# A gated attention and FFN block on one core: the last tile's second half of gate and up in other PSUM banks, and its quantised hidden rows turned by TensorE in quarters

## The reference

```python
x = x + tanh(g_xattn[0]) * cross_attention(layernorm(x), ctx, Wq, Wk, Wv, Wo, bo)   # 8 heads of 64
x = x + tanh(g_ffn[0])   * ffn(layernorm(x), w_gate, w_up, w_down)

def bitlinear(x, w):     # act_quant: rows to 127 levels by the row's largest magnitude
    return act_quant(x) @ weight_quant(w).T          # weight_quant: -1, 0, 1 times the mean magnitude
def ffn(x, w_gate, w_up, w_down):
    g = bitlinear(x, w_gate); u = bitlinear(x, w_up) # 512 -> 2048
    h = square(relu(g)) * u
    return bitlinear(h, w_down)                      # 2048 -> 512
```

## Time and profile before

| | |
|---|---|
| median of 3 runs | 1275.16 us (1270.67, 1275.16, 1582.71) |
| profiled execution, its own time | 1274.61 us |
| its span | 1272.8 us, mean granted TensorE clock 0.983 |
| busy | PE 1211.8 us (95%), DVE 1047.2 (82%), ACT 692.0 (54%), POOL 310.4 (24%) |
| DMA | 124.55 MB, mean 98 GB/s |

### The profile page before, as it was taken

One profiled execution on the slowest core, in us unless ns is written; L12 is line 12 of the kernel. 1 busy time (PEld: TensorE's weight loads), 2 busy tenths in 40 slices (PEclk: granted clock), 3 DMA queues, 4 the chain that ended last, 5 costly groups with the idle time before them and its releaser, 6 DMA issues.

```text
span 1272.8 us, 18729 instructions
## 1 busy us (share of the span) xinstructions
PE 1211.8 (95%) x6040; PEld 783.4 (62%) x6136; DVE 1047.2 (82%) x2142; ACT 692.0 (54%) x803; POOL 310.4 (24%) x299
## 2 busy tenths in 40 slices
PE   7765999999999999999999999999999999999995
PEld 5544666666666666666666666666666666666652
DVE  4967888888888888888888888888888888888873
ACT  3853455554566555554565545564575545555453
POOL 1024122222243222222243122212243222221210
PEclk9897999999999999999999999999999999999997
DMA  9740433323332344323332244322333233322322
GB/s 392 267 156 21 130 91 88 73 76 82 91 87 66 75 117 141 79 70 81 91 87 70 77 121 134 87 66 74 91 87 76 73 83 91 87 70 78 75 59 58
DMA packets 205186, 124.55 MB, mean 98 GB/s; under 512 B 173930, under 2 KB 173930, under 8 KB 202593
## 3 DMA queue, kind: packets, MB, share of 16 engines
q1 hardware_dynamic: 204573, 120.00, 34.6%
q10 hardware_dynamic: 580, 4.20, 1.1%
HBM read 57.86 MB, written 24.35 MB: 65 GB/s over the span
## 4 chain that ended last, share of the span: by engine, by line
PE 81%; DVE 5%; POOL 3%; issue 2%; ACT 2%; DMA 0%; DVEq 0%; POOLq 0%; ACTq 0%; SPq 0%
PE gu_ps L1036 32%; PE o_ps L1021 16%; PE y_ps L1049 15%; PE s_ps L56 15%; PE s_ps L1009 3%; POOL v_sb L853 1%; DVE half_max L1120 1%; POOL probs L863 1%; DVE staged L1115 1%; ACT staged L945 0%; ACT x_marked L958 0%; DVE stats L1145 0%; DVE x L1143 0%; DVE x_max L1155 0%; DVE probs L1095 0%
## 5 line engine op out<-in xcount | busy, mean ns | idle before, releaser
L1036 PE MATMUL gu_ps<-w_gate,xq_t 128*128 128x512 bf16 x990 | 238.2, 383 | 7.4 <-DVE staged L1115 4.9
L1049 PE MATMUL y_ps<-w_down,hq_t 128*128 128x512 bf16 x1023 | 233.1, 381 | 5.6 <-DMA hq_t<-staged 5.4
L1036 PE MATMUL gu_ps<-w_up,xq_t 128*128 128x512 bf16 x963 | 235.0, 380 | 3.2
L1021 PE MATMUL o_ps<-v_sb,pt_high 128*128 128x512 f32 (+1 forms) x640 | 213.9, 415 | 1.7 <-DVE pt_low L1105 1.7
L1115 DVE TENSOR_TENSOR staged<-staged,gu_ps 128x1024 f32<-128x1024 f32 x128 | 155.5, 1215 | 62.9 <-ACT staged L928 57.9
L858 POOL TENSOR_TENSOR rstd<-var_eps,neg_half 128x1 f32<-128x1 f32 x128 | 100.2, 783 | 399.6 <-DVE var_eps L1082 280.0
L958 ACT ACTIVATE x_marked<-centred,x_scale 128x512 f32<-128x512 f32 x64 | 46.2, 722 | 261.6 <-DVE x_scale L1162 261.6
L56 PE MATMUL s_ps<-a_sb,xf_high 128*128 128x308 f32 x1024 | 187.1, 305 | 0.0
L1049 PEld LDWEIGHTS y_ps<-w_down,hq_t 128*128 128x128 bf16 x1024 | 100.6, 98 | 127.9 <-issue 8.3
L1036 PEld LDWEIGHTS gu_ps<-w_up,xq_t 128*128 128x128 bf16 x1024 | 100.6, 98 | 122.3 <-issue 2.7
L56 PEld LDWEIGHTS s_ps<-a_sb,xf_high 128*128 128x128 f32 x1024 | 159.7, 188 | 5.8 <-issue 0.5
(11 more groups left out here) (106 smaller groups left out, 1431.3 us busy)
## 6 DMA issues: line engine op xcount, KB each, us to landing
xf_sb<-in_x_feat SPq DMA_DIRECT2D x64, 256.0 KB, 2.7
x_sb<-in_x_tok SPq DMA_DIRECT2D x64, 256.0 KB, 2.8
y<-staged SPq DMA_DIRECT2D x64, 256.0 KB, 2.0
staged<-in_wg_t SPq DMA_DIRECT2D x4, 1024.0 KB, 15.5
staged_up<-in_wu_t SPq DMA_DIRECT2D x4, 1024.0 KB, 23.4
staged<-in_wd_t ACTq DMA_DIRECT2D x4, 1024.0 KB, 6.8
a_scr<-a_out SPq DMA_DIRECT2D x12, 308.0 KB, 4.4
a_raw<-a_scr SPq DMA_DIRECT2D x3, 1232.0 KB, 5.7
```

Of the source, the lines that this page charges most:

```text
L1021: last = nc.tensor.matmul(o_ps[:, :], pt[0:rows, P * c:P * (c + 1)], v_sb[0:rows, v, c, :], start=(c == 0 and pt is pt_high and v == 0), s ...
L1036: last = nc.tensor.matmul(gu_ps[:, m, q, :], xq_t[:, s.par(0), c, :], w[:, c, cols], start=(c == 0), stop=(c == DC - 1))
L1049: last = nc.tensor.matmul(y_ps[:, :], hq_t[:, c, :], w_down[:, c, :], start=(c == 0), stop=(c == FC - 1))
```

## The change

In step 63 half 1 of gate goes to `s_ps` and half 1 of up to the two gate banks of `gu_ps`. The wait for DVE's multiply of half 0 is dropped; gate waits for the last reader of `s_ps` (`pt_low_done`) and up for ACT's relu of half 0 (`relu_done[0]`). ACT's relu and DVE's multiply of half 1 read from the new places.

In step 64 the hidden rows of tile 63 take another way. The constant is now `MARKED`, ROUND plus 16384, so that the low 16 bits of the float32 result hold the integer plus 16384. DVE computes three quarters of 512 columns, ACT the fourth (`mark_last`). PE transposes each quarter straight from those low halves, read as bfloat16 with a stride of two, in four 128 by 128 transposes (`turn_last`) into a bank of its own (`o_ps`, the two of `s_ps`, one of `gu_ps`). ACT takes quarters 0 and 1 and DVE quarters 2 and 3 out of PSUM as 16-bit integers, less 16384, into `hq_t` (`take_last`). PE then runs the 16 down matmuls, waiting for each quarter (`down_last`). The two DMA transposes, the two ACT and one DVE operations that took ROUND off, and the two ACT operations of 1024 columns are gone for this tile. A second identity matrix, in bfloat16, is made by POOL at the start (one more memset and one more select), 256 bytes per partition of SBUF, allocated ahead of nearly all other tiles.

```diff
+        kept.ident_b = sb("ident_b", [P, P], BF16)
...
+        last_gate_ps, last_up_ps = pt_ps, gate_ps
+        last_turned_ps = [bank[:, 0:256].bitcast(BF16) for bank in (o_ps, s_ps[:, 0, :], s_ps[:, 1, :], gu_ps[:, 1, 0, :])]
+        h_bits = h_marked[:, :].bitcast(BF16).rearrange("p (n two) -> p n two", two=2)
...
 SP
-                    if s.has(-1):
+                    if s.has(-1) and not s.opens(TILES):
                         turn_hidden(s, -1, 0)
                         turn_hidden(s, -1, 1)
...
 ACT
+                    at_end = s.opens(TILES - 1) and n == 1
+                    if at_end:
+                        act.wait_ge(square_done[0], TILES)
+                    nc.scalar.activation(relu, last_gate_ps if at_end else gate_ps, ACT.Relu).then_inc(relu_done[n], 1)
...
+                def mark_last():
+                    act.wait_ge(h_scale_done, TILES)
+                    nc.scalar.activation(h_marked[:, 1536:FFN], hidden[:, 1536:FFN], ACT.Copy, bias=MARKED,
+                                         scale=h_scale[:, 0:1]).then_inc(last_marked[3], 1)
+                def take_last(q):
+                    act.wait_ge(last_turned[q], 1)
+                    act.wait_ge(down_done, TILES - 1)
+                    nc.scalar.activation(hq_t[:, 4 * q:4 * (q + 1), :], last_turned_ps[q].bitcast(I16).rearrange("p (c n) -> p c n", c=4),
+                                         ACT.Copy, bias=-LOW_MARK).then_inc(last_ready[q], 1)
...
 PE
-                    wait(pe, hidden_done[1 - n], s.count(n))
+                    at_end = s.opens(TILES - 1) and n == 1
+                    if not at_end:
+                        wait(pe, hidden_done[1 - n], s.count(n))
...
+                        target = gu_ps[:, m, :, :]
+                        if at_end:
+                            pe.wait_ge((pt_low_done, relu_done[0])[m], TILES)
+                            target = (s_ps[:, :, :], gu_ps[:, 0, :, :])[m]
...
+                def turn_last(q):
+                    pe.wait_ge(last_marked[q], 1)
+                    for c in range(4):
+                        at = 512 * q + P * c
+                        last = nc.tensor.transpose(last_turned_ps[q][:, P * c:P * (c + 1)], h_bits[:, at:at + P, 0], ident_b[:, :])
+                    last.then_inc(last_turned[q], 1)
+                def down_last():
+                    pe.wait_ge(y_done, TILES - 1)
+                    for q in range(4):
+                        pe.wait_ge(last_ready[q], 1)
+                        for c in range(4 * q, 4 * (q + 1)):
+                            last = nc.tensor.matmul(y_ps[:, :], hq_t[:, c, :], w_down[:, c, :], start=(c == 0), stop=(c == FC - 1))
                     last.then_inc(down_done, 1)
...
 DVE
                     if s.has(1):
                         probs_low(s, 1)
+                    if s.opens(TILES):
+                        for q in range(3):
+                            mark_last(q)
                     if s.has(-2):
                         finish(s, -2)
+                    if s.opens(TILES):
+                        for q in range(2, 4):
+                            take_last(q)
```

More of the change, by code:

```diff
@@ L11 @@
 BF16 = mybir.dt.bfloat16
+I16 = mybir.dt.int16
 P = 128
@@ L45 @@
 ROUND = float(3 << 22)
+LOW_MARK = 16384.0
+MARKED = ROUND + LOW_MARK
 CENTRED_MIN = EPS * EPS**0.5
@@ L253, in _ @@
                 nc.gpsimd.memset(ident_f[:, :], 0.0).then_inc(ident_zeroed, 1)
-                pool.wait_ge(ident_zeroed, 1)
-                nc.gpsimd.affine_select(out=ident_f[:, :], in_=ident_f[:, :], compare_op=ALU.not_equal, fill=1.0, base=0,
-                                        pattern=[[-1, P]], channel_multiplier=1).then_inc(ident_ready, 1)
+                nc.gpsimd.memset(ident_b[:, :], 0.0).then_inc(ident_zeroed, 1)
+                pool.wait_ge(ident_zeroed, 2)
+                for ident in (ident_f, ident_b):
+                    nc.gpsimd.affine_select(out=ident[:, :], in_=ident[:, :], compare_op=ALU.not_equal, fill=1.0, base=0,
+                                            pattern=[[-1, P]], channel_multiplier=1).then_inc(ident_ready, 1)
                 for n in range(2):
@@ L551, in run_tiles @@
 def run_tiles(nc, x_tok, x_feat, out, a_scr, v_scr, kept):
-    ident_f, neg_half = kept.ident_f, kept.neg_half
+    ident_f, ident_b, neg_half = kept.ident_f, kept.ident_b, kept.neg_half
     w_gate, w_up, w_down, staged = kept.w_gate, kept.w_up, kept.w_down, kept.staged
@@ L660, in run_tiles @@
         down_done, y_done = sem("down_done"), sem("y_done")
+        last_marked = [sem(f"last_marked{q}") for q in range(4)]
+        last_turned = [sem(f"last_turned{q}") for q in range(4)]
+        last_ready = [sem(f"last_ready{q}") for q in range(4)]
         ones_placed = sem("ones_placed")
@@ L921, in relu_half @@
                         wait(act, weight_done, 1)
-                    nc.scalar.activation(relu, gate_ps, ACT.Relu).then_inc(relu_done[n], 1)
+                    at_end = s.opens(TILES - 1) and n == 1
+                    if at_end:
+                        act.wait_ge(square_done[0], TILES)
+                    nc.scalar.activation(relu, last_gate_ps if at_end else gate_ps, ACT.Relu).then_inc(relu_done[n], 1)
                 def square_half(s, n):
@@ L963, in step @@
                         probs_high(s, 1)
-                    if s.has(-1):
+                    if s.opens(TILES):
+                        mark_last()
+                        take_last(0)
+                        take_last(1)
+                    elif s.has(-1):
                         mark_hidden(s, -1)
@@ L1035, in gate_up @@
                             for c in range(DC):
-                                last = nc.tensor.matmul(gu_ps[:, m, q, :], xq_t[:, s.par(0), c, :], w[:, c, cols],
+                                last = nc.tensor.matmul(target[:, q, :], xq_t[:, s.par(0), c, :], w[:, c, cols],
                                                         start=(c == 0), stop=(c == DC - 1))
@@ L1051, in down @@
                     last.then_inc(down_done, 1)
+                def turn_last(q):
[10 more added lines that the diff above has]
+                            last = nc.tensor.matmul(y_ps[:, :], hq_t[:, c, :], w_down[:, c, :], start=(c == 0), stop=(c == FC - 1))
+                    last.then_inc(down_done, 1)
                 def step(s):
@@ L1063, in step @@
                         gate_up(s, 1)
-                    if s.has(-1):
+                    if s.opens(TILES):
+                        for q in range(4):
+                            turn_last(q)
+                        down_last()
+                    elif s.has(-1):
                         down(s, -1)
@@ L1114, in hidden_half @@
                     wait(dve, h_marked_done[n], s.before(0))
-                    nc.vector.tensor_tensor(hidden[:, cols], relu_sq, up_ps, ALU.mult).then_inc(hidden_done[n], 1)
+                    at_end = s.opens(TILES - 1) and n == 1
+                    nc.vector.tensor_tensor(hidden[:, cols], relu_sq, last_up_ps if at_end else up_ps,
+                                            ALU.mult).then_inc(hidden_done[n], 1)
                 def top_half(s, n):
@@ L1178, in unmark_hidden, with mark_last, take_last @@
                     nc.vector.tensor_scalar(hq[:, 0:HALF], h_marked[:, 0:HALF], -ROUND, None, ALU.add).then_inc(hq_done[0], 1)
+                def mark_last(q):
+                    dve.wait_ge(h_scale_done, TILES)
+                    dve.wait_ge(hq_done[1], TILES - 1)
+                    cols = slice(512 * q, 512 * (q + 1))
+                    nc.vector.tensor_scalar(h_marked[:, cols], hidden[:, cols], h_scale[:, 0:1], MARKED,
+                                            ALU.mult, ALU.add).then_inc(last_marked[q], 1)
+                def take_last(q):
+                    dve.wait_ge(last_turned[q], 1)
+                    dve.wait_ge(down_done, TILES - 1)
+                    nc.vector.tensor_scalar(hq_t[:, 4 * q:4 * (q + 1), :],
+                                            last_turned_ps[q].bitcast(I16).rearrange("p (c n) -> p c n", c=4),
+                                            -LOW_MARK, None, ALU.add).then_inc(last_ready[q], 1)
                 def unmark_input(s, d):
```

2 lines of the change are left out of this document (1 added, 1 removed).

## The result

| | before | changed |
|---|---|---|
| median, 9 runs each | 1275.16 us (1270.33 to 1582.71) | 1263.86 us (1259.27 to 1266.63) |
| ratio to before | 1 | 0.9921, 95% interval 0.9901 to 0.9941 |
| profiled execution, its span | 1274.61, 1272.8 us | 1259.86, 1258.0 us |

The ratio leaves out the one disturbed run of before (1582.71). A ratio of 0.9921 is 10.1 us of 1275 (7.5 to 12.6 by the interval): less than 2%, but the interval doesn't reach 1.

A forecast was written before the change was run, and what follows sets the result against it. It took the loops as a stream of matmuls (PE 95% busy), untouched by the change. In the tail, 4.4 us from the first part and 4.7 from the second sum to 9.1: 1274.61 - 9.1 = 1265.5 us, range 1261.0 to 1270.5.

The forecast's parts named there:

- First part: Half 1 of tile 63's gate and up in other banks, without waiting for DVE: `h_scale` ready 4.44 us earlier.
- Down product of tile 62, counted at nothing: Now in front of tile 63's last rows: ends at 1253.7, 0.4 us before `h_scale` is ready, so adds nothing.
- no gap would be longer than 1.1 us: PE at the end: if transposes count as work, its longest gap is 1.1 us and the full clock holds.
- Second part: Tile 63 from `h_scale` to last down matmul, marks, PE transposes and takes replacing DMA: 10.9 to 6.2 us, 4.7 saved.
- Three marks: DVE's marks of quarters 0 to 2 after `h_scale`: 0.53 us each, ending at 1.63 us.
- A quarter's transposes: Four PE transposes per quarter of tile 63: 0.1 us each, 0.4 in all, plus 0.15 until the last has landed.
- A take by DVE from PSUM: DVE takes quarters 2 and 3 behind `finish`, priced by a 687 ns pass, ending at 3.1 and 3.8 us.
- Rival A: The forecast itself: full clock through the last down product, 1265.5 us; chance 0.60.
- Rival B: Clock falls during tile 63's transposes, so its down product is some 2.1 us slower: 1267.6 us; chance 0.26.
- Rival C: Tile 63's transposes become the bound (strided loads or half clock): 3.5 us saved, 1271.1 us; chance 0.07.
- Rival D: Shifted SBUF addresses slow every loop tile; at 0.25 us per tile 7 us slower, 1281.5 us; chance 0.04.
- Rival E: Half 1 of gate doesn't start at 1245, so only 4.7 us is saved: 1269.9 us; chance 0.03.

The follow-up runs named there:

- 200 transposes: Kernel before plus second identity and 200 unused bfloat16 transposes on PE between the down products of tiles 62 and 63: one profiled run, 1277.45 us (before: 1273.02).
- run without overlap: Changed kernel, but PE waits for all four marks before the first transpose and all four takes before the first down matmul: ratio 0.9950 to before.
- part 1 alone: Changed kernel with only half 1 of gate and up in other banks; tile 63's rows go through the DMA transposes again: ratio 0.9955 to before.
- POOL is made to wait: POOL's two first-block xf_low subtractions wait for DVE's last placing: ratio to before 0.9978 on the kernel before, 0.9915 on the changed kernel.
- 52 transposes: Kernel before plus second identity and 52 unused bfloat16 transposes on PE between the down products of tiles 62 and 63: ratio 0.9972 to before.

## Why the prediction was right, point by point

The forecast was 1265.5 us with a range of 1261.0 to 1270.5; the median is 1263.86. The saving was put at 9.1 us, the traces give 9.84 for the tail, and the ratio 10.1 (7.5 to 12.6). The sum started from a profiled run with the slow start; with 9.84 it would have given 1264.8, and where the median of nine falls within the spread of the starts is chance. The profiled run of the changed kernel, 1259.86, had the quick start and lies below the range.

- **First part, 4.44 forecast, 4.56 measured**, and 4.57 by itself. The bound moved to ACT as said: unmark, relu, square, then DVE. The rest of 0.1 is that relu starts 0.94 us after the unmark starts (1242.62 to 1243.56), not the unmark's 1.04 and a gap.
- **Down product of tile 62, counted at nothing: right.** Its second half waited 1.30 us for the DMA (1.2 by the forecast's times) and ended 0.3 us before `h_scale` was ready (0.4 forecast). The prediction forgot this wait when it said that no gap would be longer than 1.1 us.
- **Second part, 4.7 forecast, 5.2 measured.** The mechanism stood; three terms were too dear. Three marks took 1.27 us and not 1.6: a pass with two steps costs 482 ns in the changed kernel, no more than one with one step, and they overlap a little. A quarter's transposes took 0.40 with the landing of the last, where 0.4 and 0.15 were forecast. A take by DVE from PSUM took 0.41 us where I took the 0.69 of a pass with two tensors, but nothing waited for it; ACT's price of 0.60 was right. The product began 2.0 us after `h_scale` was ready (near 1251.07, ready at 1249.04), against 2.5, and took 3.63, against 3.65, so the last matmul ended 5.66 us after it and not 6.2; the lower bound of the terms was 5.7. `finish` of tile 62 released it, at 1251.02, with the last transpose over at 1251.04: the two candidates came together.
- **Rival A, the full clock, held** in five profiled runs of this tail.
- **Rival B** did not occur in them. The reason given for it, that transposes are no work to the clock, is refuted by the 200 transposes: 11.33 us of them at 1.00. By the rule of the Trainium skill (TensorE: Matmul & The Clock Gate, Part 4: PE-mode transpose), as the prediction weighed it, the clock should have fallen there; it did not, and the measurement decides. But rival B's event happened where the first transpose and the product started later, and cost 1.7 us there, against the 2.1 I had put. Whether the longer idle times alone did it, or also that the short bursts between them were transposes and not plain matmuls, is not shown: both grew together in that run. How near the changed kernel is to a fall was not measured either.
- **Rival C** is out: the transposes with a stride of two columns are 0.1 us each at most, and 57 ns apart where they did not wait for marks (8 in 0.62 us, each 0.22 long, in the run without overlap). **Rival D** is out: from POOL's third normalising to `h_scale` of tile 62 it is 1105.74 us before and 1105.62 in the changed kernel, where this rival wanted 0.25 us more per tile. (A tile of the loops takes 17.8 us, not the 19 that the prediction got from PE's busy time.) **Rival E** is out by part 1 alone.
- **The range.** It was made wide at the bottom for two runs 4.5 us apart. It had to be: the times of both kernels spread over 5 to 8 us, and nearly all of that comes from the first 140 us, from the collision of DVE's copies with POOL and from half clock spells. From POOL's third normalising, near 135 us, to `h_scale` of tile 62 it is 1105.60 to 1105.74 us in eleven of the 13 profiled runs, 1106.04 in one, and 1107.03 in the one whose clock was at half at 136 us. The prediction knew the spread, not its cause; the profiled run of before (placing 3.63) and that after (1.64) fell on different sides of it. That makes 5 of the 14.8 us between them none of the change's: the second profiled run of the changed kernel has the late start too.

The timelines that show the step of the loops, POOL's normalising of one tile and the next (start first), of before and then of the changed kernel:

```profile
1010.50 1.22 POOL L863 TENSOR_TENSOR probs<-probs,prob_inv 128x616 f32<-128x616 f32 x1 [5.33 <-DVE prob_inv L1101]
1028.31 1.22 POOL L863 TENSOR_TENSOR probs<-probs,prob_inv 128x616 f32<-128x616 f32 x1 [5.33 <-DVE prob_inv L1101]
```

```profile
1005.55 1.22 POOL L877 TENSOR_TENSOR probs<-probs,prob_inv 128x616 f32<-128x616 f32 x1 [5.33 <-DVE prob_inv L1162]
1023.35 1.22 POOL L877 TENSOR_TENSOR probs<-probs,prob_inv 128x616 f32<-128x616 f32 x1 [5.33 <-DVE prob_inv L1162]
```

What stays open: what decides where the half clock spells of the start fall, and with that the 4 us spread that is left when POOL is made to wait.

## What to carry to other kernels

The last tile of a pipelined kernel has no neighbours to hide its waits, and the buffers of the stages that are over are free: give its halves banks of their own, and replace a slow transfer (here a DMA transpose of 3.26 us) by work of the engine that is idle, in pieces small enough that the next stage starts on the first. When the gain is a few microseconds, read it from one instruction ahead of the edit to one behind it in both traces, not from spans: here 5 of 14.8 us belonged to the start of the run. An idle PE can cost twice, once for the wait and once for the half clock behind it (here 1.8 us, got back by work whose result nobody reads). And before a start or a gap of PE is read from a line, compare its count of matmuls with that of the weight loads: here one record was missing, and it moved the start by 0.23 us.

## What the runs showed of the hardware

- Eight small DVE copies took 1.65 us alone (six profiled runs) and 3.63 beside two POOL subtractions of 2.50 us together (all seven in which they met).
- 128 by 128 bfloat16 transposes ran 56 ns apart (200 in 11.33 us, each 0.22 long), and kept the clock at 2.4 GHz by themselves for as long as they ran, in one run.
- A DVE pass from PSUM, 16-bit integers in and bfloat16 out, 512 columns, took 0.41 us, against 0.60 on ACT, although the two-tensor pass of float32 from PSUM takes 0.69.
- The clock fell at different times after PE stopped. In the gap of 3.9 us ahead of half 1 of tile 63, with plain matmuls on both sides, it fell 2.2 to 2.5 us after the stop in six profiled runs, and in the run with 200 transposes only 4.2 us after it, when PE was already at work again. Elsewhere it was 2.8 us behind the last of 52 transposes, and 0.9 behind the last of 16 in the run without overlap.
